# A transformer layer with eight experts on one core: the opening and the first three expert steps issued in another order

## The reference

```python
def reference(x, w_qkv, w_out, Wg, Wu, Wd, Wr, temperature):   # x: 4096 tokens x 256, f32
    h = layernorm(x); q, k, v = split(h @ w_qkv)               # 16 heads of 16
    q, k = (elu(rope(a) * 16**-0.25) + 1 for a in (q, k))
    # causal linear attention, a running state per head:
    #   kv += outer(k_t, v_t); ks += k_t; out_t = (q_t @ kv) / max(q_t . ks, 1e-6)
    x = x + out @ w_out
    h = layernorm(x)
    w = routing_weights(h, Wr, temperature)   # sigmoid, zone test, exp, top-2 fallback, normalised
    # every expert is computed for every token: 8 experts, hidden width 256
    y = sum_e w[:, e] * ((silu(h @ Wg[e]) * (h @ Wu[e])) @ Wd[e])
    return x + y
```

## Time and profile before

| | |
|---|---|
| median of 3 runs | 808.24 us (808.12 to 808.8) |
| profiled execution, first to last instruction (the span; the page gives no other time of it) | 806.5 us |
| PE busy | 760.2 us, 94% of the span |
| DVE, POOL, ACT busy | 603.2, 484.7, 465.4 us |
| mean granted TensorE clock | 0.968 of full speed |

### The profile page before, as it was taken

How to read it: one execution, slowest core, us unless ns; L and a number is a source line. 1 busy time by engine, 2 the same in 40 slices (tenths; PEclk the granted TensorE clock), 3 DMA queues, 4 the chain that set the end, 5 groups by cost and what they waited for, 6 DMA issues and landing times.

```text
span 806.5 us, 18062 instructions
## 1 busy us (share of the span) xinstructions
PE 760.2 (94%) x6660; PEld 654.1 (81%) x6660; DVE 603.2 (75%) x1596; ACT 465.4 (58%) x886; POOL 484.7 (60%) x538
## 2 busy tenths in 40 slices
PE   4475899999999999999999999999999999999997
PEld 2364688888888888888888888888888888888886
DVE  6788797878877797778877797787877787765433
ACT  3664776666566656666666556657665566534221
POOL 3785678765666665655666666566666555653232
PEclk9676799999999999999999999999999999999999
DMA  4544124122211123122101221121111121100000
GB/s 139 127 103 110 41 78 93 40 43 68 40 28 24 34 66 41 41 43 54 41 20 35 43 66 40 41 43 27 41 40 40 41 53 28 27 1 27 1 1 27
DMA packets 97319, 38.27 MB, mean 47 GB/s; under 512 B 74192, under 2 KB 96976, under 8 KB 97232
## 3 DMA queue, kind: packets, MB, share of 16 engines
...
## 4 chain that ended last, share of the span: by engine, by line
PE 88%; DVE 5%; POOL 2%; ACT 2%; issue 1%; DMA 1%; SPq 0%; DVEq 0%; ACTq 0%; POOLq 0%
PE y L446 22%; PE gate L413 22%; PE up L413 21%; PE front L288 5%; PE back L333 3%; PE front L289 3%; PE back L369 2%; PE back L344 2%; PE up L381 1%; PE front L311 1%; PE front L394 1%; PE back L326 1%; PE back L356 1%; POOL a_lo L1131 1%; PE back L311 1%
## 5 line engine op out<-in xcount | busy, mean ns | idle before, releaser
L1159 POOL TENSOR_TENSOR h_lo<-work,h_hi 128x512 fp32r<-128x512 f32 x128 | 166.3, 1299 | 66.0 <-ACT h_hi L640 66.0
L1131 POOL TENSOR_TENSOR a_lo<-am,a_hi 128x512 f16<-128x512 f32 x120 | 144.6, 1206 | 54.9 <-ACT a_hi L568 52.3
L446 PE MATMUL y<-wd_hi,h_hi 128*128 128x256 f32 x512 | 148.1, 289 | 1.7 <-DVE xa L1032 1.7
L446 PE MATMUL y<-wd_lo,h_hi 128*128 128x256 f32 x512 | 143.9, 281 | 0.0
L446 PE MATMUL y<-wd_hi,h_lo 128*128 128x256 f32 x512 | 143.8, 281 | 0.0
L1020 DVE TENSOR_TENSOR work<-work,up 128x512 f32<-128x512 f32 x128 | 87.1, 680 | 72.1 <-PE up L413 71.7
L640 ACT ACTIVATE h_hi<-work 128x512 fp32r<-128x512 f32 x128 | 80.6, 630 | 64.5 <-DVE work L1020 39.4
L1032 DVE SCALAR_TENSOR_TENSOR xa<-y,wo,xa 128x256 f32<-128x256 f32 x256 | 113.5, 470 | 4.5 <-PE y L446 4.5
L446 PEld LDWEIGHTS y<-wd_hi,h_hi 128*128 128x128 f32 x512 | 96.5, 189 | 4.9 <-issue 2.1
L446 PEld LDWEIGHTS y<-wd_lo,h_hi 128*128 128x128 f32 x512 | 96.4, 188 | 3.1
L446 PEld LDWEIGHTS y<-wd_hi,h_lo 128*128 128x128 f32 x512 | 96.4, 188 | 0.0
...
## 6 DMA issues: line engine op xcount, KB each, us to landing
...
xa<-Wg ACTq DMA_DIRECT2D x8, 256.0 KB, 2.9
work<-Wd ACTq DMA_DIRECT2D x8, 256.0 KB, 2.9
work<-Wu ACTq DMA_DIRECT2D x8, 256.0 KB, 2.8
...
qT<-q_st SPq DMA_TRANSPOSE x32, 3.2
```

The source lines that it names most:

```text
L446: m = pe.matmul(Y[t // 2][:, t % 2 * D:(t % 2 + 1) * D], h_p[hi][:, n % 2, t * P:(t + 1) * P], wd_p[wi][:, u // KI, u % KI, :], start=(n % ...
L1131: pool.tensor_tensor(a_p[1][:, heads(r), :], am_place(g, r).rearrange("p (h n) -> p h n", h=4), a_p[0][:, heads(r), :], ALU.subtract).then ...
L1159: pool.tensor_tensor(h_p[1][:, n % 2, :], hb[:, n % 2, :], h_p[0][:, n % 2, :].bitcast(F32), ALU.subtract).then_inc(s_hlo, 1)
```

## The change

Three things.

1. PE, ACT, DVE, POOL and SP have new lists for the head, and steps 5, 6 and 7 are written out too; the loop starts at `s = 8`. What the loop holds is as before, less the slab calls, of which it would have had none left.
2. Loads and splits of slabs are calls of their own. 21 slabs (0 to 20) are split by ACT before the first `silu`, the last three in steps 6 and 7. `load_slab(0)` is ACT's first instruction. On SP `load_small` (`w_out`, `Wr`, temperature) goes right behind `w_qkv`, the second table load follows the first, and `load_xa` waits for `bn(g - 4)`.
3. `tcos_scale`, which multiplies the cosine table by the tile's factor, is a `tensor_tensor` with the factor broadcast, and was a `tensor_scalar`.

```diff
-            qkv(0); qkv(1); scores(0, 0); scores(0, 1); qkv(2); av(0); state(0); scores(1, 0); o_T(0); scores(1, 1)
-            qkv(3); proj(0); av(1); scores(2, 0); state(1); x2_T(0); scores(2, 1); o_T(1); qkv(4); proj(1); av(2)
...
-            for s in range(LAG, STEPS):
+            colmean(); qkv(0); qkv(1); qkv(2); scores(0, 0); scores(0, 1); qkv(3); scores(1, 0); av(0); scores(1, 1)
+            state(0); o_T(0); proj(0); scores(2, 0); av(1); state(1); scores(2, 1); x2_T(0); o_T(1); qkv(4); proj(1)
+            scores(3, 0); av(2); scores(3, 1); x2_T(1); state(2); o_T(2); proj(2); av(3); x2_T(2); state(3); o_T(3)
+            scores(4, 0); proj(3); scores(4, 1); x2_T(3); logit_rows(0); gate(0); logit(0); av(4); qkv(5); gate(1)
+            up(0); o_T(4); state(4); gate(2); up(1); proj(4); down(0); up(2); gate(3); x2_T(4); down(1); scores(5, 0)
...
+            for s in range(8, STEPS):
                 # ACT
             def slab_hi(n):
...
-                load_slab(n + NSL - 1)
-            x_hi(0); load_slab(0); wqkv_hi(0); wqkv_hi(1)
-
-            x_hi(1); wout_hi(); qk_copy(0); v_copy(0); slab_hi(0); load_slab(1); v1(0); exp(0); k_hi(0); q_hi(0)
-            qk_copy(1); v2(0); slab_hi(1); x_hi(2); v_copy(1); v1(1); exp(1); slab_hi(2); q_hi(1); k_hi(1)
...
+            load_slab(0); wout_hi(); x_hi(0); wqkv_hi(0); slab_hi(0); wqkv_hi(1); load_slab(2); x_hi(1); wr_hi()
+            load_slab(1); load_slab(3); qk_copy(0); slab_hi(1); slab_hi(2); x_hi(2); v_copy(0); slab_hi(3); v1(0)
+            exp(0); load_slab(4); load_slab(5); k_hi(0); v2(0); q_hi(0); load_slab(6); slab_hi(4); v_copy(1)
+            qk_copy(1); x_hi(3); v1(1); slab_hi(5); load_slab(7); slab_hi(6); load_slab(8); exp(1); v2(1); slab_hi(7)
...
                 # DVE
-                v.tensor_scalar(tcos[:, :], tabs[:, g // NT % 2, g % NT, 0:HALF], rstd1[:, g % NRS:g % NRS + 1], None, ALU.mult).then_inc(s_tcos, 1)
+                v.tensor_tensor(tcos[:, :], tabs[:, g // NT % 2, g % NT, 0:HALF],
+                                rstd1[:, g % NRS:g % NRS + 1].broadcast_to([P, HALF]), ALU.mult).then_inc(s_tcos, 1)
+            setup_first(); w_sum(); wout_lo(); bn(0); x_lo(0); mean_var(0); wc(0); wc(1); wqkv_lo(0); bn(1)
+            wqkv_lo(1); var_eps(0); mean_var(1); var_eps(1); tcos_scale(0); bn(2); mean_var(2); bn(3); x_lo(1)
...
+            k_lo(4); ln2(2); o_sum(3, 0); o_sum(3, 1); den_max(3); den_rec(3); norm(3); var_eps(6); x2_lo(2)
+            slab_lo(17); o_lo(3); st_add(3); tcos_scale(5); mask(4, 0); x1_add(3); wr_lo(); bn2(3); mean_var2(3)
+            var_eps2(3); mean_var(7); mask(4, 1); ln2(3); x2_lo(3); mask(4, 2); mask(4, 3); route_sum(0)
+            route_zone(0); slab_lo(20); route_nearest(0); o_sum(4, 0); o_sum(4, 1); cos(5); den_max(4); den_rec(4)
+            norm(4); var_eps(7); rope(5); h_up(0); phi(5); o_lo(4); tcos_scale(6); route_weight(0); h_up(1); k_lo(5)
...
                 # POOL
-            setup_first()
-            for g in range(NT):
-                rstd1_pow(g)
-            sin(0, 1); sin(0, 0); slab_lo(0); v_rest(0); sin(1, 1); sin(1, 0); v3(0); slab_lo(1); v_rest(1)
...
+            setup_first(); rstd1_pow(0); rstd1_pow(1); slab_lo(0); sin(0, 1); sin(0, 0); slab_lo(1); v_rest(0)
+            rstd1_pow(2); slab_lo(3); v3(0); slab_lo(4); sin(1, 1); sin(1, 0); v_rest(1); rstd1_pow(3); slab_lo(6)
+            slab_lo(7); v3(1); sin(2, 1); sin(2, 0); a_lo(0, 0); a_lo(0, 1); a_lo(0, 2); a_lo(0, 3); slab_lo(9)
+            slab_lo(10); sin(3, 1); sin(3, 0); st_rest(0); a_lo(1, 0); a_lo(1, 1); s3(0); rstd1_pow(4); a_lo(1, 2)
+            a_lo(1, 3); v_rest(2); slab_lo(12); v3(2); rstd2_pow(0); a_lo(2, 0); slab_lo(13); st_rest(1); v_rest(3)
+            a_lo(2, 1); a_lo(2, 2); a_lo(2, 3); s3(1); sin(4, 1); sin(4, 0); rstd2_pow(1); a_lo(3, 0); a_lo(3, 1)
+            v3(3); slab_lo(15); st_rest(2); a_lo(3, 2); s3(2); a_lo(3, 3); rstd2_pow(2); slab_lo(16); v_rest(4)
...
                 # SP, load_xa
+                w.wait_ge(s_bn, g - 3)
...
-            load_wqkv(0); load_wqkv(1)
-            load_xr(0); load_xa(0); load_xr(1)
...
+            load_wqkv(0); load_wqkv(1); load_small(); load_xa(0); load_xr(0); load_xr(1); load_xa(1); load_tab(0)
+            load_tab(1); load_xa(2); load_xa(3); load_xa(4); load_xr(2); load_xr(3); transpose_q(0); transpose_k(0)
+            load_xr(4); load_xr(5); load_xa(5); load_xa(6); load_xa(7); transpose_k(1); transpose_q(1); load_xa(8)
...
```

More of the change, by code:

```diff
@@ L41 @@
 NSL = 3
-HEAD_SLABS = 12
-STEP_SLABS = 4
 STEPS = NTL + LAG + 1
@@ L648, in scalar_program @@
[L648 to L652, removed]
@@ L654, in scalar_program @@
+            a_hi(7, 0); h_hi(10); a_hi(7, 1); x_hi(8); s2(6)
+            for s in range(8, STEPS):
                 a, c, n = s, s - 1, NT * (s - LAG)
                 router = (s - LAG) // NT if (s - LAG) % NT == 0 else -1
[L656 to L658 removed]
@@ L1043, in vector_program @@
[L1043 to L1047, removed]
@@ L1048, in vector_program @@
-            rope(3); mask(2, 1); den_rec(1); mean_var(5); norm(1); x_lo(4); phi(3); x2_lo(0); mask(2, 2); mask(2, 3)
-            q_lo(3); tcos_scale(4); o_lo(1); k_lo(3); cos(4); x1_add(1); bn2(1); mean_var2(1); var_eps2(1)
-            o_sum(2, 0); o_sum(2, 1); ln2(1); den_max(2); slab_lo(8); den_rec(2); st_add(2); wr_lo(); norm(2)
-            mask(3, 0); mask(3, 1); x2_lo(1); rope(4); o_lo(2); mask(3, 2); mask(3, 3); phi(4); x1_add(2); bn2(2)
-            mean_var2(2); var_eps2(2); k_lo(4); q_lo(4); o_sum(3, 0); o_sum(3, 1); ln2(2); den_max(3); den_rec(3)
@@ L1053, in vector_program @@
-            norm(3); x_lo(5); x2_lo(2); o_lo(3); st_add(3); x1_add(3); bn2(3); mean_var2(3); var_eps2(3); mask(4, 0)
-            ln2(3); mask(4, 1); var_eps(5); x2_lo(3); slab_lo(11)
-            for s in range(LAG, STEPS):
+            setup_first(); w_sum(); wout_lo(); bn(0); x_lo(0); mean_var(0); wc(0); wc(1); wqkv_lo(0); bn(1)
+            wqkv_lo(1); var_eps(0); mean_var(1); var_eps(1); tcos_scale(0); bn(2); mean_var(2); bn(3); x_lo(1)
+            var_eps(2); cos(0); tcos_scale(1); rope(0); mean_var(3); rtemp_first(); slab_lo(2); phi(0); var_eps(3)
@@ new lines, in vector_program @@
+            x_lo(2); bn(4); q_lo(0); k_lo(0); cos(1); slab_lo(5); mean_var(4); rope(1); phi(1); x_lo(3); mask(0, 0)
+            mask(0, 1); k_lo(1); q_lo(1); tcos_scale(2); mask(0, 2); ones_vx(); cos(2); rope(2); mask(0, 3)
+            slab_lo(8); x_lo(4); phi(2); tcos_scale(3); mask(1, 0); mask(1, 1); var_eps(4); o_sum(0, 0); o_sum(0, 1)
+            den_max(0); den_rec(0); st_add(0); norm(0); q_lo(2); k_lo(2); o_lo(0); cos(3); mask(1, 2); mask(1, 3)
+            x1_add(0); rope(3); bn2(0); slab_lo(11); mean_var2(0); phi(3); mask(2, 0); mask(2, 1); o_sum(1, 0)
@@ new lines, in vector_program @@
+            var_eps2(0); o_sum(1, 1); bn(5); tcos_scale(4); den_max(1); ln2(0); st_add(1); den_rec(1); k_lo(3)
+            norm(1); mask(2, 2); q_lo(3); mask(2, 3); mean_var(5); o_lo(1); x2_lo(0); bn(6); rtemp_half(); var_eps(5)
+            slab_lo(14); mean_var(6); x1_add(1); cos(4); bn2(1); mean_var2(1); var_eps2(1); mask(3, 0); mask(3, 1)
+            o_sum(2, 0); o_sum(2, 1); rope(4); den_max(2); ln2(1); den_rec(2); mask(3, 2); norm(2); x_lo(5); st_add(2)
+            phi(4); x2_lo(1); o_lo(2); mask(3, 3); bn(7); q_lo(4); x1_add(2); bn2(2); mean_var2(2); var_eps2(2)
@@ new lines, in vector_program @@
+            tcos_scale(7); st_add(5); acc(2, 3); x1_add(5); bn2(5); mean_var2(5); h_up(6); var_eps2(5); mask(6, 0)
+            ln2(5); mask(6, 1); mask(6, 2); mask(6, 3); x2_lo(5); acc(4, 0); h_up(7); acc(4, 1); cos(7); o_sum(6, 0)
+            o_sum(6, 1); den_max(6); acc(4, 2); den_rec(6); acc(4, 3); rope(7); h_up(8); phi(7); norm(6); slab_lo(23)
+            k_lo(7); var_eps(8); acc(6, 0); q_lo(7); acc(6, 1); acc(6, 2); o_lo(6); h_up(9); st_add(6); x1_add(6)
+            bn2(6); mean_var2(6); var_eps2(6); ln2(6); acc(6, 3); mask(7, 0); h_up(10); mask(7, 1); x2_lo(6); h_up(11)
```

95 lines of the change are left out of this document (50 added, 45 removed).

## The result

The changed kernel takes 816.26 us (814.96 to 817.06, 4 runs) against 808.18 for the kernel before on the same chip: ratio 1.0102, 95% interval 1.0088 to 1.0116. Forecast were 804.7 us, and 799.5 to 811.0 for the range. It is 8 us slower, the interval lies clear of 1, and the prediction is wrong in sign. The profiled execution has a span of 814.8 us (before 806.5).

What follows compares the result with a forecast made beforehand. PE was taken to bound the kernel from 202 us on, the head being a chain with DVE nearest to full. Head -0.9, steps 5 to 7 -2.6, rest 0: -3.5 from 808.24 gives 804.7 us, range 799.5 to 811.0.

Steps and rivals of the forecast that it cites:

- Part 3 (d): First tile in the head: av(0) at about 39 against some 34.5 us, DVE work done level within 1 us at 41.24.
- Part 4: Head's limit: POOL's idle halves, av(3) at 71.3, chain 9.7 us, x2_lo(3) ends at 81.0; head gives 0.9 us.
- The walk: First tile followed through the head's new lists: exp(0) at 20.5, scores(0) at some 29, av(0) at about 39 us.
- the rule that stands beside it: Start of the head: DMA engines serve queues round-robin by packet, so load_slab(0) beside w_qkv costs 0.9 us, not 0.5.
- Part 3 (e): Head after av(0): new order better laid out, qkv(3) and qkv(4) earlier; 5.0 us of DVE's waits were for qk_copy.
- Part 2: More split work in the head: DVE +3.3 us to 64.2, POOL +7.7 to 58.4, ACT +4.4.
- Rival D: POOL becomes the head's bound and its time is slower: x2_lo(3) at 86.0, total +2.5 us, 810.7; chance 0.26.
- Part 5: Steps 5 to 7: PE's wait for norm(4) and the lower clock after it go, gaining 2.6 of 3.6 us.
- The bound of 0: Steps 5 to 7, least gain forecast: 0 us, if another wait takes the place of the one for norm(4).
- Part 1: Cosine table's tcos_scale as tensor_tensor: frees 0 to 0.7 us of DVE in the head, 0.4 taken; loop worth 0.

Runs made afterwards that it cites:

- the hold: Changed kernel with POOL waiting, after each rstd2_pow of tiles 0 to 7, until that tile's ln2 is done; 813.57 us, ratio 1.0067 to before.
- the two with the misplaced filling: Changed kernel, the hold, unused matmuls in PE's waits, one awaiting v_copy(4): 818.09 us; twin with slabs 12-23 split in steps 5-7: 826.01 us.

## Why the prediction was wrong, step by step

**The failed step is Part 3 (d) and the two terms of Part 4 that hang on it.** The walk itself was good: w_sum at 5.91 (0.45 late; 0.5 was taken, and 0.9 by the rule that stands beside it), scores(0, 0) at 29.43 ("some 29"), av(0)'s products with a_lo from 38.53 on (39 was said). The prediction knew that av(0) would be four us late. It let that go because in DVE work done at 41.24 the orders were level, and Part 4 then had the delay made up: POOL would idle only 3.3 us between av(0) and av(3), half of what it did, and the chain from av(3) to the end of x2_lo(3) would take 9.7 us. The window from av(0) to av(3) of the kernel after (columns as in the earlier trace rows; POOL is the fifth engine):

```profile
38.53:75.06 36.53, 20.14 (x301) 16.18 (x297) 32.72 (x77) 21.99 (x48) 30.32 (x34) 0.64 0.35 82
```

POOL worked 30.3 us (29 was said) and idled 6.2, not 3.3: av(3)'s products with a_lo began at 75.06 instead of 71.3. The chain behind them took 12.85 us instead of 9.7. The two make up the 6.9 us between the forecast 81.0 and the measured 87.9. Set against the kernel before, the 6.1 us of the head are 3.9 at av(0), 0.5 from there to av(3), and 1.6 in the chain behind av(3), which the hold brings back to 11.2 (11.3 before). Nothing made up av(0)'s delay, and the run with a delayed tile 0 shows the same for the old order.

DVE had indeed done 29.14 us by 41.24, 2.15 more than before. But that was work for tiles 2 to 4 and slabs; the head's end hangs on tile 0's chain and a cadence of 27 us that did not shrink. In twelve kernels, the one before among them, with x2_lo(0) starting anywhere from 53.0 to 63.6, the cadence was 25.7 to 27.7 us (the changed kernel: 28.7; the two with the misplaced filling are left out). Part 3 (e) came true and did not help: of DVE's 6.2 us of waits for qk_copy after 34 us none is left.

**Part 2's volume was priced without what it does to its neighbours.** From w_sum to the end of x2_lo(3) DVE worked 69.6 us, 8.7 more than before, where 3.3 had been counted, and idled 12.8 instead of 15.4. DVE's instructions got longer as POOL's list closed up: ln2 alone 3.0 us in the head (4.6 against 1.6), six slab_lo 5.2 where 4.2 had been priced, tcos once 1.00, den_max once 1.01. The earlier trace rows held the warning, a 0.41 us instruction once at 1.47; I used it for the cosine edit and nowhere else. POOL's part was also miscounted: eight of its slab_lo stand in the head before, not six, so four more were added and not six; POOL's 58.4 us came out at 59.9 all the same. Rival D's signs came, POOL's idle above all, of 6.2 us (6.7 in the window of the earlier trace rows, 6.8 from av(0) itself at 34.60 to av(3)), and x2_lo(3) past 84. Its +2.5 was still too small, because it priced neither the longer DVE instructions nor a loss in steps 5 to 7.

**Part 5: -2.6 was forecast, +2.0 came.** The windows from logit_rows(0) to gate(12), before and after, and the first 15 us of the latter:

```profile
82.00:155.21 73.21, 70.56 (x603) 59.72 (x604) 60.26 (x150) 50.36 (x95) 53.19 (x57) 0.95 0.31 69
```

```profile
88.06:163.29 75.23, 71.69 (x603) 58.66 (x604) 57.39 (x138) 47.22 (x87) 43.08 (x46) 0.97 0.21 45
88.06:103.50 15.44, 15.44 (x128) 12.03 (x129) 8.66 (x25) 11.67 (x23) 7.49 (x8) 0.84 0.06 18
```

The wait for norm(4) went, as forecast (PE is busy for the whole of the first 15.4 us), and from 103.5 us on the clock is full. But after that PE waits in other places, 3.5 us in all where it had waited 2.65 before: 0.91 for a silu, 0.66 and 0.63 for h_up, 0.63 for a transpose. The other 1.1 us of the 2.0 are PE busy longer with the same instructions; why, is open. The bound of 0 should have reached below nothing; the run with norm(4) ahead shows on the old kernel that moving it can cost more than it gives. For one of these waits the cause can be seen. Three router instructions of 128x32 (two additions and a multiplication) that took 0.19, 0.19 and 0.41 us in the kernel before took 1.05, 1.24 and 1.08 in a row, each beside a POOL instruction of 1.2 us, and h_up behind them let PE wait:

```profile
112.93 1.05 DVE L991 TENSOR_TENSOR router<-router 128x32 f32<-128x32 f32 x1
114.01 1.24 DVE L997 TENSOR_TENSOR router<-router 128x32 f32<-128x32 f32 x1
115.28 1.08 DVE L999 TENSOR_TENSOR router<-router 128x32 f32<-128x32 f32 x1
```

```profile
117.11 0.71 PE L403 MATMUL up<-x_hi,wu_hi 128*128 128x512 f32 x2 [0.63 <-DVE work L1019]
```

With the hold steps 5 to 7 still take 74.6 us, 1.35 more than before; PE is busy as long as before there (70.6 us) and waits 3.9.

**Part 1: 0.4 was forecast for the head, and nothing came.** In the loop the tcos takes as long in either form, as the Trainium skill's rule beside my value says (SBUF — State Buffer, who interferes with whom: two SBUF inputs contend with GpSimd as a two-port mode does). In the head of the old order the new form did save 0.75 us of DVE, and the time stayed; in the head of the changed kernel the first five took 2.6 us, more than before, with the 1.00 among them.

**Held:** no change from step 8 on; the clock below 0.8 from 41.24 to 82 us (0.59; up to 41.24 it was 0.90, which was not foreseen); exp(0) later than before, if by 1.0 and not 1.8 us (19.67).

**Sum:** 4.4 (tile 0) + 1.7 (cadence; 1.5 given back by the hold) + 2.0 (steps; 0.7 given back) = 8.1 us. Open are two things. The first is which of its steps makes tile 0 late; none was tried alone. The trace shows the delay growing: the transpose of k for tile 0 is issued 1.3 us later (24.63 and 23.36) and lets PE start scores(0, 0) 2.7 us later (29.43 and 26.77), in a stretch with more DMA traffic (173 GB/s against 119); mask(0, 0) starts 2.2 us later (30.34 and 28.13); a_lo(0, 0) 3.3 us later (33.13 and 29.88), behind slabs, v3(1) and sin(2) on POOL; and the last a_lo waits for mask(0, 3), which stands behind others' work on DVE (35.65 and 30.78). The second is what each of PE's waits in steps 5 to 7 is worth; the one behind the router instructions is the only one followed to its cause.
